# Flamingo block, first cross-attention: x and context loaded in halves, the second halves of both turned inside the head loop

## The reference

```python
def _L0_xattn_ref(k, v, q, ssm_kernel, D, head_dim):      # k = v = ctx, q = layernorm(x)
    kv = jnp.einsum('bhil,bhjl->bijhl', k_, v_)           # 8 x 8 products per head, over time
    y = irfft(rfft(kv, n=2 * L) * rfft(ssm_kernel, n=2 * L))[..., :L]   # causal convolution in time
    out = y + kv * D
    out = jnp.einsum('bijhl,bhil->bjhl', out, q_)
x = x + jnp.tanh(g_xattn[0]) * _L0_xattn_ref(ctx, ctx, _layernorm(x), ssm_kernel, D, 8)
x = x + jnp.tanh(g_ffn[0]) * _L0_ffn_ref(_layernorm(x), w1, b1, w2, b2)      # int8-quantised FFN
x = x + jnp.tanh(g_xattn[1]) * _L1_xattn_ref(...)
x = x + jnp.tanh(g_ffn[1]) * _L1_ffn_ref(...)                                # ternary weights
```

## Time and profile before

| what | us |
|---|---|
| median of 3 runs (lowest, highest) | 692.77 (688.34, 695.46) |
| the profiled execution, its own time | 694.3 |
| its span, first to last instruction | 692.5 |
| first head starts on TensorE | 33.94 |
| last of 32 heads starts on VectorE | 203.94 |
| TensorE busy in the span | 622.8 |

### The profile page before, as it was taken

One profiled execution on the slowest core, in us unless ns is written; L12 is line 12 of the kernel. 1 busy time (PEld: TensorE's weight loads), 2 busy tenths in 40 slices (PEclk: granted clock), 3 DMA queues, 4 the chain that ended last, 5 costly groups with the idle time before them and its releaser, 6 DMA issues.

```text
span 692.5 us, 9580 instructions
## 1 busy us (share of the span) xinstructions
PE 622.8 (90%) x2859; PEld 367.7 (53%) x2859; DVE 547.5 (79%) x1075; ACT 484.1 (70%) x730; POOL 356.5 (51%) x438
## 2 busy tenths in 40 slices
PE   2699999979998089897999999999988899999997
PEld 1677777767777044453444555555543344444443
DVE  5646888886796848995678778889999999999965
ACT  2835666657637468899663446656768999999985
POOL 2457789886866364220000100002347988988961
PEclk9999999999999569998999999999999999999999
DMA  7937789899970016305709930000111665665651
GB/s 280 387 133 244 256 274 321 247 253 375 371 223 1 0 73 231 121 0 192 295 26 170 222 103 0 0 0 0 31 31 62 173 176 169 177 186 172 202 157 46
DMA packets 123475, 110.48 MB, mean 160 GB/s; under 512 B 83168, under 2 KB 90096, under 8 KB 122288
## 3 DMA queue, kind: packets, MB, share of 16 engines
q1 hardware_dynamic: 116864, 97.42, 46.6%
q10 hardware_dynamic: 6576, 12.67, 5.6%
HBM read 61.75 MB, written 28.39 MB: 130 GB/s over the span
## 4 chain that ended last, share of the span: by engine, by line
PE 70%; DVE 12%; POOL 5%; issue 4%; ACT 4%; DMA 3%; SPq 1%; POOLq 0%; DVEq 0%
PE ps L1130 18%; PE ps L1362 13%; PE ps L1236 8%; PE ps L1378 8%; PE ps L1200 4%; PE ps L1289 4%; PE ps L1319 3%; PE ps L1269 2%; PE ps L1274 2%; PE ps L1282 2%; PE ps L1293 2%; DVE hmax L1615 2%; PE ps L1337 1%; DVE turn L1528 1%; DVE ps L1524 1%
## 5 line engine op out<-in xcount | busy, mean ns | idle before, releaser
L1130 PE MATMUL ps<-arena 128*128 128x288 f32 x640 | 161.3, 414 | 8.8 <-POOL arena L540 6.6
L1130 PEld LDWEIGHTS ps<-arena 128*128 128x128 f32 x640 | 122.9, 194 | 44.3 <-issue 5.6
L1362 PE MATMUL ps<-arena 128*128 128x512 bf16 x512 | 113.9, 380 | 4.3 <-DVE arena L1896 3.9
L636 POOL TENSOR_TENSOR arena<-arena 128x512 f32<-128x512 f32 x64 | 80.3, 1274 | 9.0 <-DVE arena L1896 8.1
L1362 PEld LDWEIGHTS ps<-arena 128*128 128x128 bf16 x512 | 49.5, 98 | 66.5 <-DVE arena L1896 4.3
L539 POOL TENSOR_TENSOR arena<-arena 128x1024 f32<-128x1024 f32 x32 | 60.6, 1893 | 15.1 <-PE ps L1130 9.3
L1518 DVE TENSOR_TENSOR turn<-ps,arena 128x768 f32<-128x768 f32 x32 | 30.6, 957 | 42.8 <-PE ps L1130 31.0
L1236 PE MATMUL ps<-arena 128*128 128x512 bf16 x256 | 58.3, 392 | 3.6 <-DVE arena L1676 2.7
L1200 PE MATMUL ps<-arena 128*128 128x512 bf16 (+1 forms) x256 | 58.8, 389 | 2.0 <-ACT arena L866 1.4
L1378 PE MATMUL ps<-arena 128*128 128x512 bf16 x256 | 58.2, 380 | 1.6 <-ACT arena L1027 0.7
L546 POOL TENSOR_TENSOR turn<-turn 128x512 f32<-128x512 f32 x32 | 42.5, 1327 | 27.1 <-DVE turn L1528 27.0
(11 more groups left out here) (215 smaller groups left out, 1314.4 us busy)
## 6 DMA issues: line engine op xcount, KB each, us to landing
arena<-in_L_ffn_w SPq DMA_DIRECT2D x48, 512.0 KB, 5.8
arena<-kpad_d ACTq DMA_DIRECT2D x16, 512.0 KB, 6.5
hq_d<-arena SPq DMA_DIRECT2D x14, 512.0 KB, 3.1
tern_d<-late SPq DMA_DIRECT2D x24, 256.0 KB, 6.0
arena<-in_x SPq DMA_DIRECT2D x4, 1024.0 KB, 9.5
arena<-in_ctx SPq DMA_DIRECT2D x4, 1024.0 KB, 17.3
arena<-in_L_ffn_w ACTq DMA_DIRECT2D x8, 512.0 KB, 4.8
x_d<-arena SPq DMA_DIRECT2D x4, 1024.0 KB, 4.2
```

Of the source, the lines that this page charges most:

```text
L636: pool.tensor_tensor(hg[:, s, sl], hh[:, s, sl], g3[:, sl], ALU.mult).then_inc(S["hg_done"], 1)
L1130: last = pe.matmul(ps[:, 4 * s + lo, 0:NB * PAIRS], toep[:, u, (LB - 1 - lo + li) * P:(LB - lo + li) * P], kv[:, s, li, :], start=(li == 0 ...
L1362: last = pe.matmul(ps[:, bank, :], xq4T[:, s, 4 * j + k, :], w[:, k, c * L:(c + 1) * L], start=(k == 0), stop=(k == LB - 1))
```

## The change

- SyncE loads the first half of x (eight tiles in `order1`), the first half of the context, then the second half of x and the second half of the context. The two small gate loads follow the first halves.
- Ahead of the heads only the eight first tiles of x are normalised (two by ScalarE, six by VectorE) and turned, along with the eight first tiles of the context. The statistics of the second half of x are still taken there, by VectorE.
- ScalarE normalises the second eight x tiles into a new buffer `xlate` at 144 to 160 KB of the arena, four in iteration 0 and four in iteration 1.
- Every head from 0 to 15 turns a late tile: context in heads 0 to 7, x in heads 8 to 15. `late_copy` copies it out after the product of its head.
- Before `repeat_q(16)`, the first that reads the second half of q, ScalarE copies the tiles of heads 14 and 15.
- `xlate` shares its memory with fw1T, where the DMA transposes of w1 land. They therefore wait for head 15, and move from iterations 14, 18, 22 and 27 of the stream to 18, 20, 24 and 27.
- The magnitude sums run two an iteration in 2 to 13, in place of 12 in seven iterations from 0 to 13. The Tanh of the gates and the second Toeplitz load move back in ScalarE's order.

The diff, cut to its core:

```diff
+        xlate = cut(144, 8 * L).rearrange("p (s l) -> p s l", s=8)
...
-            return range(12 * h // 7, 12 * (h + 1) // 7) if h < 14 else ()
+            return range(2 * h - 4, 2 * h - 2) if 2 <= h < 14 else ()
...
-            for g in range(NG):
-                sp.dma_start(x_res[:, G * g:G * g + G, :], x_rows[:, G * g:G * g + G, :]).then_inc(rows_in[g], 16)
+            for half in range(2):
+                for g in range(2 * half, 2 * half + 2):
+                    sp.dma_start(x_res[:, tiles_of(g), :], x_rows[:, tiles_of(g), :]).then_inc(rows_in[g], 16)
+                for g in range(2 * half, 2 * half + 2):
+                    sp.dma_start(ctx_nat[:, G * g:G * g + G, :], ctx_rows[:, tiles_of(g), :]).then_inc(c_in[g], 16)
...
+                sp.wait_ge(S["y_ready"], HEADS // 2 + 2)
                 sp.dma_start_transpose(fw1T[:, :, m * L:(m + 1) * L].bitcast(I16),
...
-                    if k % 2 == 0 and k:
-                        w1_turned(k // 2 - 1)
+                    if k in (4, 5, 7):
+                        w1_turned((k - 3) // 2 if k > 4 else 0)
...
+            def late_copy(h):
+
+                act.wait_ge(S["prod_done"], h + 3)
+                m, ready = (ctxT, "c_out") if h < NT // 2 else (qT, "q_out_act")
...
             for h in range(HEADS - 2):
+                if h + 1 == HEADS // 2:
+                    late_copy(h - 1)
+                    late_copy(h)
+                    act.wait_ge(S["q_out_act"], G + NT // 2)
                 repeat_q(h + 1, 1 - h % 2)
...
-                if CTX_LATE < h <= CTX_LATE + NT // 2:
-                    ctx_late(h - 1 - CTX_LATE)
+                if 1 <= h < HEADS // 2 - 1:
+                    late_copy(h - 1)
+                if h < 2:
+                    for n in range(NT // 2 + G * h, NT // 2 + G * h + G):
+                        x_normal(n, xlate[:, n - NT // 2, :])
...
             q_tiles(0)
+            c_tiles(0)
+            c_tiles(1)
             q_tiles(1)
-            c_tiles(0)
-            q_tiles(2)
-            c_tiles(1)
-            q_tiles(3)
...
+                if h < NT // 2:
+                    late = ctx_nat[:, NT // 2 + h, :]
+                    if h % G == 0:
+                        pe.wait_ge(c_in[2 + h // G], 16)
+                else:
+                    late = xlate[:, h - NT // 2, :]
+                    xn0_made(pe, h)
```

More of the change, by code:

```diff
@@ L514, in norm_scales @@
                     pool.wait_ge(ready, g)
-                for sem_used, each in used:
+                for sem_used, counts in used:
                     if g >= 2:
-                        pool.wait_ge(sem_used, each * (g - 1))
+                        pool.wait_ge(sem_used, counts[g - 2])
                 po.done(pool.tensor_tensor(nmean[:, :], mv2[:, u, :, 0], neg1[:, :], ALU.mult))
@@ L522, in norm_scales, with norm_x0 @@
                 pool.tensor_tensor(shift2[:, u, :], nmean[:, :], rstd2[:, u, :], ALU.mult).then_inc(ready, 1)
-            for g in range(NG):
-                norm_scales(g, S["rs0"], S["st0"], ((S["xn0_act"], 2), (S["xn0_dve"], 2)))
+            def norm_x0(g):
+                norm_scales(g, S["rs0"], S["st0"], ((S["xn0_act"], (2, 2)), (S["xn0_dve"], (2, 6))))
+            norm_x0(0)
+            norm_x0(1)
             def w1_scale(n):
@@ L721, in _ @@
             act.dma_start(kpad_d, kpad[:, :]).then_inc(S["k_stored"], 16)
-            act.wait_ge(S["gate_in"], 32)
-            act.activation(tg[:, :], gates[:, :], ACT.Tanh).then_inc(S["tanh_done"], 1)
             act.wait_ge(S["k_stored"], 16)
             toep_load(0, 0)
+            x_normal(0, x0[:, 0, :])
+            x_normal(1, x0[:, 1, :])
+            for n in range(G):
+                c_copy(n)
             toep_load(1, 1)
[L727 to L732, removed]
-                if g >= 2:
-                    for n in range(G * (g - 2), G * (g - 1)):
-                        c_copy(n)
+            q_copy(1)
+            q_copy(3)
+            for n in range(G, 2 * G):
+                c_copy(n)
             def repeat_c(h, u):
@@ L744, in _ @@
             repeat_c(0, 0)
-            for t in range(NT - 3, NT, 2):
-                q_copy(t)
+            q_copy(5)
+            q_copy(7)
             repeat_c(1, 1)
-            act.wait_ge(S["q_out_dve"], NT // 2)
-            act.wait_ge(S["q_out_act"], NT // 2)
+            act.wait_ge(S["gate_in"], 32)
+            act.activation(tg[:, :], gates[:, :], ACT.Tanh).then_inc(S["tanh_done"], 1)
+            act.wait_ge(S["q_out_dve"], G)
+            act.wait_ge(S["q_out_act"], G)
             def repeat_q(h, u):
@@ L1096, in q_tiles @@
             def q_tiles(g):
-                for t in range(G * g, G * g + G):
-                    xn0_made(pe, t)
-                    if t >= 4:
-                        pe.wait_ge(S["q_out_act" if t % 2 else "q_out_dve"], t // 2 - 1)
+                for n in range(G * g, G * g + G):
+                    xn0_made(pe, n)
+                    if n >= 4:
+                        pe.wait_ge(S["q_out_act" if n % 2 else "q_out_dve"], n // 2 - 1)
                     for l in range(LB):
-                        last = pe.transpose(ps[:, 4 + t % 4, l * P:(l + 1) * P], x0[:, t % 8, l * P:(l + 1) * P], identf[:, :])
+                        last = pe.transpose(ps[:, 4 + n % 4, l * P:(l + 1) * P], x0[:, n, l * P:(l + 1) * P], identf[:, :])
                     last.then_inc(S["q_tr"], 1)
```

122 lines of the change are left out of this document (62 added, 60 removed).

## The result

The changed kernel takes 697.5 us in the median (694.3 to 700.67, 14 runs), the kernel before 692.37 us in the same series (686.0 to 696.17, 14 runs). The ratio is 1.0078, 95% interval 1.0054 to 1.0102: 5.4 us slower, between 3.7 and 7.1 us. The forecast was 695.1 us, within a range of 687.5 to 703.5 us; as a difference it was 2.3 us. The profiled execution has a span of 697.2 us against 692.5.

What follows compares the result with a forecast made beforehand. TensorE, busy 622.8 of 692.5 us, was taken as the bound, through when it starts heads and how evenly. Terms -5.8 + 3.9 + 2.3 + 1.9 + 0 = +2.3 us on 692.8 gave 695.1 us, range 687.5 to 703.5.

Steps and rivals of the forecast that it cites:

- Head 0 earlier, 5.8 us: At the start, TensorE's head 0 begins near 27.7 us, 6.2 us earlier; less 0.4 us for its late tile, gain 5.8 us.
- Sixteen late tiles, 3.9 us: Heads 0 to 15, with sixteen late tiles for eight, take 83.2 us in place of 79.35, 3.9 us more.
- Two steps as before: Within heads 0 to 15, two steps between heads stay unchanged, 10.57 us together.
- Work given to ScalarE, nothing: Eight normalisations in iterations 0 and 1, and two sums an iteration, are covered and priced at nothing.
- The wait ahead of head 17, 2.3 us: Both last q tiles must be out before repeat_q(16), so TensorE loses 2.3 us ahead of head 17.
- the clock, 1.9 us: After the idle time ahead of head 17 the granted clock drops, charged at 1.9 us; the other end is 0.
- just fits: The Toeplitz load for heads 18 and 19, some 6 us later, has about 6.7 us; the median landing suffices.
- The transposes, nothing: Three w1 transposes for two between iterations 18 and 24 cost 0; the other end is a second stall, 5.4 us.
- keep the stall of head 22 as it is: The DMA stall at head 22, an interval of 10.24 us, was assumed to stay unchanged.
- rival 1: Head 22's stall goes, as its Toeplitz load lands in time: -3.1 us, 689.7 us; chance 0.18.
- rival 2: A second DMA stall from close transposes or a missed load for heads 18 and 19: +7.7 us, 700.5 us; chance 0.22.
- The sum, +2.3 us: Whole kernel: all terms together make it 2.3 us slower, a median of 695.1 us; chance 0.47.

Runs made afterwards that it cites:

- e4: The changed kernel with all of x loaded ahead of the context again; 700.27 us, ratio 1.0123 to the kernel before.
- e6: The changed kernel with TensorE's wait for the third context load moved inside head 0, ahead of its late tile; 695.9 us, ratio 1.007 to the kernel before.
- e5: The changed kernel with ScalarE's late copy ahead of repeat_q and repeat_c in iterations 1 to 14; 691.03 us, ratio 0.9985 to the kernel before.
- e2: The changed kernel with repeat_c(17) ahead of the copy of tile 15 in iteration 15; 692.55 us, ratio 1.0005 to the kernel before.
- e3: The changed kernel with the first three w1 transposes issued one iteration later, behind the Toeplitz loads; 693.3 us, ratio 1.0006 to the kernel before.
- e1: The kernel before with only its first three w1 transposes moved, to iterations 18, 20, 24 from 14, 18, 22; 693.03 us, ratio 1.0014.
- e9: The changed kernel without turning the eight late x tiles, so the second half of q is not turned; 687.21 us, ratio 0.9943 to the kernel before.
- e10: The kernel before with its w1 transposes of iterations 18 and 22 issued one iteration later, behind the Toeplitz load; 688.74 us, ratio 0.9952.
- e8: The changed kernel with e3, e5, e6, and repeat_c(17) and both loads of iteration 15 ahead of tile 15's copy; 682.04 us, ratio 0.9859 to the kernel before.

## Why the prediction was right, step by step

*Head 0 earlier, 5.8 us.* Measured 6.5 us on VectorE. The limit was the one named, the third context load, at 27.05 us for 27.7. The pairs had been placed at 26.6 to 27.8 us and were ready at about 25.8 us: TensorE did the 32 context transposes in 4.07 us, nearly all at the faster of the two rates by which I had bounded them. The granted clock does not explain these rates: it stands at 1.00 over the slow transposes of the earlier trace rows as over the fast ones, and what does was not tried. e4 and e6 show the two limits apart.

*Sixteen late tiles, 3.9 us.* The mechanism was right and the size low: 4.9 us. Two parts are mis-sized. "Two steps as before" is wrong for the second: head 2 now waits for a late copy, because late tiles begin with head 0, and takes 5.80 us for 5.29. And the slow steps of the rest are 5.91 us in place of 5.79 in most cases. e5 shows that both hang on the time of the copy: with it first, all steps are 5.29 us. Why the slow step grew by 0.12 us was not tried.

*Work given to ScalarE, nothing.* Held: in e5 the heads up to 14 run at 5.29 us, TensorE's pace, with all of it in place.

*The wait ahead of head 17, 2.3 us, and the clock, 1.9 us.* Measured 2.41 us of idle time and 6.84 us for a head of 4.85, 2.0 us. e2 takes both away and returns 4.38 us. The clock's part is a frequent outcome, not a certain one: the drop came in the changed kernel, e3, e5 and e6, and not in e4, after the same idle time. What decides it is not shown. To charge it in full because 2.3 us lies nearer to 3.10 than to 1.07 was a guess that came true in four profiles of five. That ScalarE's late Toeplitz load "just fits" held only because head 17 was late; e2, with head 17 on time, shows it 1.0 us late.

*The transposes, nothing.* e1 leaves it between 1.0 us of gain and 3.0 us of loss. The premise "keep the stall of head 22 as it is" was the weak step: the stall varies from profile to profile. In the eight profiles with a transpose ahead of the Toeplitz load of iteration 19 that step took 5.66, 5.82, 6.77, 8.04, 9.09, 9.84, 10.83 and 12.02 us, besides 10.24 us in that of before, and 4.85 us in the three with the order turned. In the profile of the changed kernel rival 1, in which it goes by chance, did not happen, though in e1 and e4 the step came close to that; rival 2, a second stall, did not either. In these nine profiles the load behind the transpose landed after 10.0 to 14.1 us, in the other three after 6.1 to 6.4 us, although the two stand in different queues; the load at 165.13 us of the kernel before, behind its own transpose and landed after 7.0 us, is the exception. The Trainium skill (DMA: Bandwidth & Descriptors, Queues, rings and completion order) has the engines serve the queues in turn, packet by packet; taken as a promise that the load is hardly delayed, it does not fit the nine landings, only the exception. And its 261 GB/s for a transpose (same page, Latency and other measured facts) does not fit landings of 10.0 to 14.8 us for 0.52 MB in the changed kernel.

*The sum, +2.3 us.* Heads 0 to 31 gave +3.4 us: 0.7 us better at the start, 1.0 us worse in the late tiles, 0.2 and 0.6 us worse in the two stretches behind. The medians give +5.4 us with an interval from 3.7 to 7.1. The direction is settled, and so are the terms of the late tiles and of the wait (e2, e5, e9). The gap of some 2 us between the profile's heads and the medians stays open. Part of it may be the term of the transposes: by the medians the order of transpose and load costs the changed kernel 5.0 us (e3) and the kernel before 3.3 us (e10), but the intervals are wider than that difference. As a difference 5.4 us were measured for 2.3 forecast. The range, some 8 us either way, held that easily, so it is the terms that bear the prediction out and not the number. One profile against one profile carries the draws of the stall and of the stretch behind the heads, each a few microseconds wide.

## What to carry to other kernels

Moving work from a prologue into a pipelined loop is paid at the loop's slowest hand-over, not at its busy time: 0.45 us of TensorE a tile became 0.75 us a head because a copy stood third in ScalarE's order, and moving it first gave 4.2 us back. Where the moved work must be complete before something reads it, look at what else stands behind that wait on the same engine; here one repeat_c out of order gave back 4.4 us. And a load on whose landing TensorE waits is safer ahead of a DMA transpose in time, even if the two are in different queues: behind it, nine loads here were late and one was not.

## What the runs showed of the hardware that was not expected

A DMA transpose of 0.5 MB issued by SyncE 0.9 us ahead of a 0.5 MB load on ScalarE's queue (2.2 us in e2) went with a landing of that load after 10.0 to 14.1 us in nine profiles, against a median of 6.5 us over all such loads before; with the transpose issued 2.7 us behind it, the load landed after 6.1 to 6.4 us in three. The one load elsewhere in the kernel before that stands 0.9 us behind a transpose landed after 7.0 us. After nearly the same idle time of TensorE (2.41 us in the changed kernel, 2.42 us in e4) the granted clock was 0.66 in the window behind it and 1.00; after 3.44 and 3.47 us of idle time at the start it was 0.64 in the window of head 0's start in e8 and 1.00 in e6. And 16 transposes of the same form took 3.65 us and 1.91 us in the kernel before, both under a granted clock of 1.00.
